# A Mamba layer and a mixture of experts on one core: index loads without their check, the expert tiles' rows requested by ScalarE, eight buffers for the final sum

## The reference

```python
x = _layernorm(x + _L0_attn_ref(x, ...))     # 2 x 2048 x 128: Mamba
x = _layernorm(x + _L0_ffn_ref(x, ...))      # the experts
def _L0_ffn_ref(x, Wg, bg, W1, b1, W2, b2):  # D = 128, H = 512, E = 8, K = 2
    scores = softmax(xt @ Wg + bg)
    topk_probs, topk_idx = top_k(scores, K)
    eo = gelu(xt @ W1[e] + b1[e]) @ W2[e] + b2[e]      # for every expert e
    return sum over k of topk_probs[k] * eo[topk_idx[k]]
```

## Time and profile before

| | |
|---|---|
| median of 3 runs (821.9 to 824.73) | 822.85 us |
| the profiled execution's own time | 822.21 us |
| its span, first to last instruction | 820.4 us |
| busy: PE / DVE / ACT / POOL | 614.9 / 672.7 / 428.9 / 561.6 us |
| mean granted TensorE clock | 0.895 |
| DMA over the span | 117.39 MB, 60390 packets, mean 143 GB/s |
| hardware queue of SP (q1) | 54560 packets, 107.20 MB |

### The profile page before, as it was taken

The page is one execution under the profiler, slowest core; times in us unless marked ns, Lnnn a source line. Parts: engine busy times, 40 slices in busy tenths (PEclk is TensorE's granted clock), DMA queues, the critical chain, the costliest instruction groups (busy, mean ns, idle before and its releaser), DMA issues. The chain is left out here.

```text
span 820.4 us, 12590 instructions
## 1 busy us (share of the span) xinstructions
PE 614.9 (75%) x3055; PEld 294.4 (36%) x3071; DVE 672.7 (82%) x1349; ACT 428.9 (52%) x886; POOL 561.6 (68%) x538
## 2 busy tenths in 40 slices
PE   9777889889877887887886747774319988888900
PEld 4322223323222222222321212211318878878800
DVE  4298999999999999999989999997326777777754
ACT  3757685765666567468474543341105444444424
POOL 4355876868888898899797789777644554444533
PEclk9889999999999999999997887767559999999965
DMA  3195384685589576576557548640036556555555
GB/s 89 42 215 129 85 197 103 163 189 125 135 206 259 119 165 144 138 164 161 116 133 166 117 110 198 149 102 27 27 105 160 171 163 172 163 171 161 162 153 167
DMA packets 60390, 117.39 MB, mean 143 GB/s; under 512 B 8816, under 2 KB 37296, under 8 KB 52256
## 3 DMA queue, kind: packets, MB, share of 16 engines
q1 hardware_dynamic: 54560, 107.20, 54.2%
q0 software_dynamic: 4320, 8.99, 3.4%
q10 hardware_dynamic: 1440, 0.40, 0.2%
HBM read 100.21 MB, written 16.35 MB: 142 GB/s over the span
## 5 line engine op out<-in xcount | busy, mean ns | idle before, releaser
L550 POOL TENSOR_TENSOR hc<-hs,Crep 128x1024 f32<-128x1024 f32 x128 | 300.8, 2357 | 95.1 <-DVE hs L1379 75.0
L1379 DVE TENSOR_TENSOR_SCAN hs<-bank,state,flow 128x512 f32<-128x512 f32 x256 | 312.7, 1266 | 16.8 <-ACT bank L1122 10.6
L1122 ACT ACTIVATE bank<-bank,negA 128x512 f32<-128x512 f32 x256 | 164.1, 659 | 184.1 <-PE bank L795 183.1
L795 PE MATMUL bank<-delta,sel 64*128 64x512 f32 x512 | 159.0, 700 | 84.4 <-DVE hs L1379 84.1
L1362 DVE TENSOR_TENSOR flow<-flow,bank 128x2048 f32<-128x2048 f32 x63 | 142.7, 2265 | 0.0
L1263 ACT ACTIVATE flow<-bank,b1T 128x128 f32<-128x128 f32 x284 | 81.1, 368 | 83.1 <-PE bank L985 75.3
L795 PEld LDWEIGHTS bank<-delta,sel 64*128 64x128 f32 x512 | 42.5, 201 | 178.4 <-DVE hs L1379 145.8
L985 PE MATMUL bank<-flow 128*128 128x128 f32 x568 | 81.8, 288 | 15.6 <-issue 12.6
L670 POOL DMA_INDIRECT results<-flow,idn x71 | 69.8, 983 | 33.7 <-issue 33.7
L804 PE MATMUL bank<-hc,kc 128*32 128x512 f32 x512 | 74.7, 658 | 9.9 <-POOL hc L550 9.9
L985 PEld LDWEIGHTS bank<-flow 128*128 128x128 f32 x568 | 70.4, 195 | 28.5 <-issue 20.1
(11 more groups left out here) (193 smaller groups left out, 795.7 us busy)
## 6 DMA issues: line engine op xcount, KB each, us to landing
flow<-du_d SPq DMA_DIRECT2D x63, 1024.0 KB
flow<-L_ffn_W SPq DMA_DIRECT2D x71, 256.0 KB
xg<-xs SPq DMA_DIRECT2D x71, 66.0 KB
hs<-results SPq DMA_DIRECT2D x16, 256.0 KB, 4.4
du_d<-du SPq DMA_DIRECT2D x28, 128.0 KB
xin<-L_attn_x SPq DMA_DIRECT2D x8, 256.0 KB, 3.0
out<-hc SPq DMA_DIRECT2D x8, 256.0 KB, 2.6
results<-flow,idn POOLq DMA_INDIRECT x71
```

The lines of the kernel that those rows point to most:

```text
L550: nc.gpsimd.tensor_tensor(hc[:, Q % 2, two, :], hs[:, Q % 2, two, :], Crep[u % 3][:].unsqueeze(1).broadcast_to([P, 2, T]), ALU.mult).then_ ...
L795: ins = nc.tensor.matmul(dbank[2 * odd + i][:], sel[rows, odd, q % 4, :], delta[u % 2][rows, q // 4, :])
L1122: nc.scalar.activation(dbank[G % 4][:], dbank[G % 4][:], ACT.Exp, scale=negA[:, ch:ch + 1]).then_inc(s_ex, 1)
L1379: nc.vector.tensor_tensor_scan(hs[:, Q % 2, j, :], dbank[G % 4][:], flow[Q % 3][:, j, :], state[:, Q // QUADS % 2, Q % QUADS, j:j + 1], AL ...
```

## The change

Four edits.

1. A helper `index` takes the place of `value_load`: the same `TENSOR_LOAD`, without the two instructions that check the bounds. It is used on SP (`tail`, `etab`), TensorE, VectorE and ScalarE.
2. `load_tile` moves from SP's program to ScalarE's. ScalarE waits for the lists (the same semaphores), requests tiles 0, 1 and 2, and then in turn n requests tile n+3 ahead of the gelu of tile n. SP's expert loop holds W1 alone.
3. The final sum has eight pairs of buffers in place of four (`hs`, `pre`, `relu`, `rest`, all idle by then), a semaphore of its own for each unit's load, and SP requests all eight units' loads ahead of the first store.
4. In the final sum a token's place is (p, t): partition p holds tokens 4p to 4p + 3 of the unit, in the loads and in the store, which makes pieces of 2048 bytes.

```diff
+        def index(entry, engine, most):
+            return nc.values_load(entry, engines=(engine,), min_val=0, max_val=most,
+                                  skip_runtime_bounds_check_because="the tables are made on the chip within these bounds")
...
-        ycomb = hs[:].rearrange("p a j t -> p (a j) t").rearrange("p (r k) (t d) -> p r k t d", k=2, t=TT)
+        ycomb = [hs[:, a, 2 * r:2 * r + 2, :].rearrange("p k (t d) -> p k t d", t=TT) for a in range(2) for r in range(2)]
+        ycomb += [pre[:, 2 * r:2 * r + 2, :].rearrange("p k (t d) -> p k t d", t=TT) for r in range(2)]
+        ycomb += [room[:].rearrange("p k (t d) -> p k t d", t=TT) for room in (relu, rest)]
...
             def load_w1(n):
-                e = sp.value_load(etab[0:1, n:n + 1], min_val=0, max_val=E - 1)
+                e = index(etab[0:1, n:n + 1], mybir.EngineType.SP, E - 1)
                 after(sp, e_h, n - 3)
...
-            for n in range(3):
-                load_tile(n)
-            for n in range(MAXT):
-                if n >= 3:
-                    load_w1(n)
-                if n + 3 < MAXT:
-                    load_tile(n + 3)
+            for n in range(3, MAXT):
+                load_w1(n)
...
             def load_sum(u):
-                after(sp, c_1, u - 3)
                 for k in range(2):
-                    sp.dma_start(ycomb[:, u % 4, k], results[bass.ds(NTOK * k + T * u, T), :]
-                                 .rearrange("(t p) d -> p t d", p=P)).then_inc(c_in[u % 4], 16)
+                    sp.dma_start(ycomb[u][:, k], results[bass.ds(NTOK * k + T * u, T), :]
+                                 .rearrange("(p t) d -> p t d", p=P)).then_inc(c_in[u], 16)
...
-            for u in range(4):
+            for u in range(UNITS):
                 load_sum(u)
             for u in range(UNITS):
                 store(u)
-                if u + 4 < UNITS:
-                    load_sum(u + 4)
...
+            def load_tile(n):
+                r = index(rtab[0:1, n:n + 1], mybir.EngineType.Activation, E * REGION + E - 1)
+                after(act, e_xT, n - 7)
+                after(act, e_ob, n - 7)
+                act.dma_start(xg[:, n % 8, :], xs[bass.ds(r * P, P), :]).then_inc(e_g[n % 8], 16)
+
             act.wait_ge(s_plan, 14)
+            act.wait_ge(s_fill, 16)
+            act.wait_ge(s_tail, 16 * E)
+            for b in range(B):
+                act.wait_ge(s_scat[b], 128 * (UNITS // 2))
+            for n in range(3):
+                load_tile(n)
             for n in range(MAXT):
-                gelu(n, act.value_load(etab[0:1, n:n + 1], min_val=0, max_val=E - 1))
+                if n + 3 < MAXT:
+                    load_tile(n + 3)
+                gelu(n, index(etab[0:1, n:n + 1], mybir.EngineType.Activation, E - 1))
```

More of the change, by code:

```diff
@@ L328, in mamba_moe @@
         e_sc = [sem(f"results_scattered{r}") for r in range(8)]
-        c_in = [sem(f"results_loaded{r}") for r in range(4)]
+        c_in = [sem(f"results_loaded{u}") for u in range(UNITS)]
         c_1 = sem("pair_added")
@@ L445, in _ @@
             for e in range(E):
-                r = sp.value_load(tail[0:1, e:e + 1], min_val=0, max_val=(E * REGION - 1) * P)
+                r = index(tail[0:1, e:e + 1], mybir.EngineType.SP, (E * REGION - 1) * P)
                 sp.dma_start(xs[bass.ds(r, P), :], fills[:, e, :]).then_inc(s_tail, 16)
@@ L450, in load_w1 @@
             def load_w1(n):
-                e = sp.value_load(etab[0:1, n:n + 1], min_val=0, max_val=E - 1)
+                e = index(etab[0:1, n:n + 1], mybir.EngineType.SP, E - 1)
                 after(sp, e_h, n - 3)
                 sp.dma_start(w1r[n % 4], W1.rearrange("e d h -> (e d) h")[bass.ds(e * P, P), :]).then_inc(e_w[n % 4], 16)
[L455 to L459, removed]
             for n in range(3):
                 load_w1(n)
[L463 to L466, removed]
-            for n in range(3):
-                load_tile(n)
-            for n in range(MAXT):
-                if n >= 3:
-                    load_w1(n)
-                if n + 3 < MAXT:
-                    load_tile(n + 3)
+            for n in range(3, MAXT):
+                load_w1(n)
             def load_sum(u):
-                after(sp, c_1, u - 3)
                 for k in range(2):
-                    sp.dma_start(ycomb[:, u % 4, k], results[bass.ds(NTOK * k + T * u, T), :]
-                                 .rearrange("(t p) d -> p t d", p=P)).then_inc(c_in[u % 4], 16)
+                    sp.dma_start(ycomb[u][:, k], results[bass.ds(NTOK * k + T * u, T), :]
+                                 .rearrange("(p t) d -> p t d", p=P)).then_inc(c_in[u], 16)
             def store(u):
                 sp.wait_ge(s_fin, u + 1)
-                sp.dma_start(out[u % 2, bass.ds(u // 2 * T, T), :].rearrange("(t p) d -> p t d", p=P),
+                sp.dma_start(out[u % 2, bass.ds(u // 2 * T, T), :].rearrange("(p t) d -> p t d", p=P),
                              final[u % 4]).then_inc(s_out[u % 4], 16)
@@ L1002, in _ @@
                 if n < MAXT:
-                    chosen[n] = pe.value_load(etab[0:1, n:n + 1], min_val=0, max_val=E - 1)
+                    chosen[n] = index(etab[0:1, n:n + 1], mybir.EngineType.PE, E - 1)
                     x_T(n)
@@ L1563, in _ @@
                 if n < MAXT:
-                    chosen[n] = dve.value_load(etab[0:1, n:n + 1], min_val=0, max_val=E - 1)
+                    chosen[n] = index(etab[0:1, n:n + 1], mybir.EngineType.DVE, E - 1)
                     x_evac(n)
@@ L1571, in add_pair @@
             def add_pair(u):
-                dve.wait_ge(c_in[u % 4], 32 * (u // 4 + 1))
+                dve.wait_ge(c_in[u], 32)
                 after(dve, s_fin, u - 3)
-                nc.vector.tensor_tensor(total[u % 4], ycomb[:, u % 4, 0], ycomb[:, u % 4, 1], ALU.add).then_inc(c_1, 1)
+                nc.vector.tensor_tensor(total[u % 4], ycomb[u][:, 0], ycomb[u][:, 1], ALU.add).then_inc(c_1, 1)
                 dve.wait_ge(c_1, u + 1)
```

## The result

| | before | after |
|---|---|---|
| median | 822.51 us (4 runs, 821.9 to 824.73) | 791.98 us (4 runs, 791.02 to 794.3) |
| ratio, 95% interval | | 0.9628, 0.96 to 0.9657 |
| the profiled execution's own time | 822.21 us | 794.3 us |
| its span | 820.4 us | 792.5 us |

The account below looks back on a forecast made before the run. SP's queue, requesting each tile's W1 and rows, was taken to bound the expert stage, with VectorE close behind. Savings of 23.2 us (experts), 0.2 (start) and 5.0 (final sum) made 28.4, giving 794.4 us; range 787 to 809.

Parts of the forecast that it names:

- The bound before: Expert stage: SP's queue never waits, needs 2.2 us a tile for two requests, and sets the pace of 2.346.
- VectorE's check, 0.28: Expert stage: dropping the check's two instructions saves VectorE 0.28 us a turn, between 0.21 and 0.44.
- 1.89: Expert stage: VectorE's turn in us without its check, 2.17 less 0.28.
- TensorE, 1.97: Expert stage: TensorE needs 1.97 us from one transpose to the next, in a turn where nothing held it back.
- ScalarE's queue, 1.8: Expert stage: with the rows' requests added, ScalarE's queue needs 1.8 us a tile, between 1.7 and 1.95.
- 2.00 a tile: Expert stage: us a tile after the change, bounds 1.90 and 2.20; over 67 tiles 23.2 us less.
- a ring of queues that wait for each other: Expert stage: TensorE, VectorE and ScalarE, within 0.2 us, don't reach the largest's 1.97 exactly, so 2.00 a tile.
- rival "rows are late": Expert stage: ScalarE's queue or its rows are late, 2.2 us a tile and 807.8 us in all; chance 0.17.
- W1's 2.91: Expert stage: us from a W1's issue to its first product; a 256 KB transfer is not there earlier.
- The final sum, 5.0: Final sum: 4.3 us less from VectorE's pace of 2.19 a unit, 0.7 at the first unit; 4.3 to 5.6.
- The start, 0.2 less: Start of the expert stage: one check fewer ahead of the first rows, 0.2 us less.
- Slower (0.04): Expert stage: ScalarE's DMA waits for the four activations, 2.5 us a tile and 828 us in all; chance 0.04.

Follow-up runs that it names:

- run 1: The changed kernel with the bounds checks back on every engine's index load; ratio to the kernel before 0.992, 2.234 us a tile.
- run 2: The changed kernel with the tiles' rows requested by SP again, all index loads unchecked; ratio to the kernel before 0.9643, 1.907 us a tile.
- run 5: The changed kernel with the bounds check back on VectorE's index load alone; ratio to the kernel before 0.9859, 2.182 us a tile.
- run 6: The changed kernel with the bounds checks back on ScalarE's two index loads alone; ratio to the kernel before 0.9898, 2.236 us a tile.
- run 7: The changed kernel with the last of four pieces of every tile's second product left out; ratio to the kernel before 0.9619, 1.853 us a tile.
- run 8: The changed kernel with rows requested by SP, idle TensorE products and Gelu's table loaded ahead of the first tile; ratio to the kernel before 0.9588.
- run 10: The changed kernel with rows requested by SP, unchecked, measured again on the chip of the repeated changed kernel; 789.01 us, ratio to before 0.9601.
- run 9: The changed kernel, unaltered, measured again on another chip; 791.53 us, ratio to the kernel before 0.9628.

## Why the prediction was right, step by step

**The bound before.** Right in its mechanism: a queue that never waits and runs at the pace of the stage was the limit, SP's. Runs 1 and 2 take SP's load away in two ways, and both times SP waits and the stage is faster. SP's checks were not taken away alone; runs 5 and 6 let expect some 2.2 us a tile of it, an estimate.

**VectorE's check, 0.28.** Right: 0.28 in after, and 0.28 again in run 5. The turn that followed was not. 1.89 had been worked out from a turn that held the longer form of line 1556's operation, and 1.73 is what VectorE needs without it.

**TensorE, 1.97.** Too high by 0.07. The row that "nothing held back" was held back a little, since after shows 1.90 for the same work. Seventeen passes of 0.11 us need 1.90, and run 7 shows that this is the bound.

**ScalarE's queue, 1.8.** 1.73 measured, inside 1.7 to 1.95. A DMA request costs ScalarE 0.34 us, as it costs SP. The index load took ScalarE 0.28 to 0.29 us in the median, and 0.40 to 0.43 in the three kernels with the rows on SP (runs 2, 8 and 10). The floor of some 600 ns that the Trainium skill states in "DMA: Bandwidth & Descriptors", Latency and other measured facts, does not hold in this loop, and ScalarE's turn of 1.73 us, which holds two of them, agrees. One sign did not come: the gelu was to be released by the product and not by "issue", and the profile of after names the product 38 times and "issue" 29 times. That ScalarE's queue, at 1.73, is at times still full where TensorE needs 1.90 would explain it, and was not tried.

**2.00 a tile.** Right as a number (1.99 and 1.98), by luck: its reason was wrong. The prediction put what lies above its longest queue on a ring of queues that wait for each other. The ring reaches its longest queue exactly, 1.90 in the median. What lies above it is a few long turns: rows that are late (3.8 of the 6.4 us in after), and one turn at which VectorE stands still (1.7). TensorE's term was 0.07 too high, the waiting between the queues was put at 0.03 and is nothing, and the 0.1 of long turns was no term at all. They met in the right sum.

**The rival "rows are late" (0.17).** It was turned down with "66 KB should not land later than W1's 2.91". That step failed, and with it a sign that the prediction had named as proof of being wrong came true: transposes wait for rows. Most land in time for a use 3.5 us later, but some don't, and TensorE waited 3.8 us for them in after and 3.2 in run 9. It was worth 2 to 4 us and not 13, because few turns were hit. The 2.91 itself was no floor: W1s of before were used 2.53 us behind their request.

**The rule that spreading requests over engines saves only issue time, usually small** (the Trainium skill, "DMA: Bandwidth & Descriptors", Issuing engines are not separate DMA queues). Before, it was not small: two checked requests filled SP's queue. Once the checks were gone it was, and run 2 shows that the move then brings nothing. The prediction had booked the move as what frees SP ("It loses a request of 1.10 us a tile and a check"). Either of the two edits alone frees SP. But only the checks also free VectorE and ScalarE, which stood 0.05 to 0.1 us a tile behind it.

**The final sum, 5.0.** 4.7 measured, with 3.45 for 3.3 at the first unit and 2.21 for 2.19 as pace. The share of the piece size (1.2 to 2.3 of 4.7) was not foreseen. The upper bound of 5.6 should have read 5.4 by its own rows (4.3 and 3.99 - 2.91).

**The start, 0.2 less.** 0.7 more. Tile 0's transpose came 0.5 us earlier, but the clock rose some 4 us later. From tile 0 to tile 3 it took 7.6 us in run 9 and 9.4 in the first execution of the same kernel, so this differs by some 2 us from one execution to the next, and the change did not cause it.

**Slower (0.04).** Excluded: ScalarE's DMA is issued while the four activations run (674.96, inside 674.09 to 675.23).

## What to carry to other kernels

A loop whose engines all load an index per turn pays for its bounds check on every engine's own queue, 0.2 to 0.3 us each. The checks run side by side, so most of the gain comes only when the last of them goes: here all checks together cost 0.24 us a tile (run 1), VectorE's alone 0.19 and ScalarE's two alone 0.24. Look at a queue that never waits before you look at the engines, and when you free it, work out every other queue's turn, for the next one may be 0.1 us behind. When a transfer's request is moved to a queue that waits for data, its lead shrinks; request it so many turns ahead that the lead in us, and not in tiles, is what it was.

## What the runs showed of the hardware

- A bounds check on a register takes two instructions, 0.15 and 0.02 us on ScalarE, 0.18 and 0.02 on VectorE, and costs the queue 0.23 and 0.28 us with the gaps around them.
- VectorE's fp32 product of 128 x 128 in SBUF took 0.29 us, and 0.38 to 0.52 if it started 0.5 to 0.6 us behind the start of GpSimd's indirect DMA (0.98 us); it then ended 1.01 to 1.02 us behind that start, in 181 of 181 cases. The turn's other operations on 128 x 128 kept their duration.
- A DMA on ScalarE's queue is issued in 0.34 us and waits for no activation ahead of it.
- TensorE's granted clock, 0.50 in the 18 us without work, was 0.84 from 604 to 606 us with idle products since 601 us (run 8). With the first tiles' work alone, from 611 us on, it was 1.00 from 616 to 620 us in run 9 and 0.50 in the first execution of the same kernel.
